# Mixing product of a two-layer kernel: 16 matmuls with 128 weight columns, two at a time, for 32 on 64 by 64, four at a time

## The chip, the cores and the metric

The kernel runs on one core of one Trainium2 chip. The metric is the time of one execution on the device in microseconds (us), where lower is better. Times of instructions come from one profiled execution, recorded by the hardware profiler. An instruction is named by its line in the kernel before: L595 is line 595.

## What is computed

x has the shape (64, 64, 1024): 64 examples, 64 channels, 1024 positions. Two layers are added to it, each of a small condition-dependent product followed by a large one along the positions.

```python
x = x + _L0_ffn_ref(_L0_cond_ref(x, cond_128, ...), L0_ffn_weight)
x = x + _L1_ffn_ref(_L1_cond_ref(x, cond_128, ...), L1_ffn_W, ...)
...
def _L1_cond_ref(x, embedding, W0, b0, W1, b1, W2, b2, weight, bias_k):
    ...
    att = jax.nn.softmax((h @ W2 + b2) / T, axis=-1)
    agg_w = jnp.einsum('bk,koi->boi', att, weight[..., 0])
    agg_b = att @ bias_k
    out = jnp.einsum('boi,bih->boh', agg_w, x) + agg_b[:, :, None]
    return out
```

Layer 0 is a grouped convolution over the positions with a bias from the condition, and an int8-quantised product with a 1024 by 1024 weight. Layer 1 mixes the 64 channels of each example with a 64 by 64 matrix of its own, agg_w[b], and multiplies the result along the positions with a second 1024 by 1024 weight, to which a gated rank-32 product is added. The change is in the mixing, the last einsum that is shown.

## The kernel before

A tile is two examples: 128 partitions (example e of the pair on partitions 64e to 64e + 63, one channel each) by 1024 positions, and there are NT = 32 tiles. The kernel is written out by hand: each engine has one instruction list, and semaphores join the lists. No scheduler moves anything, so the order of the calls in the block of the tensor engine is the order of the work on it.

The block of the tensor engine (from L470) has three parts. The first, to L772, prepares weights and starts the first tiles. The second is the loop of L781, with steps c from 3 to 31. A step has, in this order, the convolution of tile c (`conv`, L541, in float32 for c below 6; `split_conv`, L516, in float16 from there on), the mixing of tile c - 3 (`mix`, L583), the int8 product of tile c - 2 (`int_product`, L611), which is interrupted by small transposes and sums (L620, L624, L564, L691), then the transposes of tile c - 1 (L580) and in every second step a rank product for two tiles (L651 and L656). The third part, from L827, has the last three mixings between pieces of the large product of layer 1 (`dense`, L708), and then the rest of that product for all tiles (L908 and L890), with no mixing in it.

The array of the tensor engine is used in several forms. The profile writes a form as rows*columns: 128*128 is the whole array (L611, L580, L708, L908), 128*64 uses two column halves, one matmul in each (the first half of `split_conv`), 64*64 uses four quarters (the second half of `split_conv`, and `mix`). The quarter follows from the partitions that the operands lie on and from those that the result goes to.

`mix(t)` computes for each example e of the tile the product of x (64 channels by 1024 positions, tile `x1`) with agg_w transposed (64 by 64, tile `mixT`). x1 is the operand that is loaded as weights, and mixT is the one that streams, so that the result comes out with the positions on the partitions, as the large product needs it. For each of 8 blocks k of 128 positions there are four matmuls, for j = 0, 1 (halves of the block, 64 positions each) and e = 0, 1. The result of example e goes to PSUM bank 2 + e, on partitions 64j to 64j + 63. All operands are float32. A float32 matmul stands in the profile as two records, each with its own load of weights, so a `mix` has 32 calls, 64 matmul records and 64 load records; the kernel has 32 of them.

`mix` waits for x1 (`x1_ready`) and for the banks to have been emptied by the scalar engine (`hi_ready`, in the last three tiles `lo_ready`). Its last matmul raises `mix_ready`, on which the scalar engine copies the two banks out.

Of the kernel before, what the change touches and what calls it, by code (L numbers as in the profile page):

```python
# [15 lines left out]
P = 128  # L16
B, CH, L = 64, 64, 1024
# [44 lines left out]
def program(nc, x, x_phases, conv_taps, pack, w_nat, w_rows, w_q, mix_w, mix_rows, w_b, b_ffn, out):  # L62
    ctx = ExitStack()
    with ctx:
        ctx.enter_context(nc.allow_non_contiguous_dma(reason="small weights"))

        def sb(name, shape, dt):
            return ctx.enter_context(nc.sbuf_tensor(name, shape, dt))
# [3 lines left out]
        def sem(name):  # L72
            if name not in sems:
                sems[name] = ctx.enter_context(nc.semaphore(name))
            return sems[name]

        def wait(eng, name, val):
            if val > 0:
                eng.wait_ge(sem(name), val)
# [12 lines left out]
        mixT = mix_home[:, 0:NT * CH].rearrange("p (t o) -> p t o", t=NT)  # L92
# [17 lines left out]
        x1 = sb("x1", [P, 2, L], F32)  # L110
# [96 lines left out]
        def bank(n, k=1):  # L207
            return ps[:, n * 512:(n + k) * 512]
# [262 lines left out]
        def _(pe):  # L471
            mm, tr = nc.tensor.matmul, nc.tensor.transpose
# [110 lines left out]
            def mix(t):  # L583
                if t == 0:
                    pe.wait_ge(sem("agg_ready"), 4)
                wait(pe, "x1_ready", 2 * t + 2)
                if t <= KEPT:
                    wait(pe, "hi_ready", 2 * t)
                else:
                    pe.wait_ge(sem("lo_ready"), 2 * (t - KEPT))  # L590
                for k in range(NL):
                    for j in range(2):
                        for e in range(2):
                            b, l = slice(e * CH, (e + 1) * CH), k * P + j * 64
                            last = mm(bank(2 + e)[j * 64:(j + 1) * 64, k * CH:(k + 1) * CH], x1[b, t % 2, l:l + 64], mixT[b, t, :],  # L595
                                      start=True, stop=True)
                last.then_inc(sem("mix_ready"), 2)

            def int_product(t, h, lo=0, hi=PH):
# [120 lines left out]
            for g in range(GRP):  # L720
                last = mm(ps_small[:, 128 + g * B:128 + (g + 1) * B], pk[:, PACK["w_ctx"]][:, g * P:(g + 1) * P],
                          pk[:, PACK["condT"]], start=True, stop=True)
# [52 lines left out]
            j = 0  # L775
# [5 lines left out]
            for c in range(3, NT):  # L781
# [6 lines left out]
                if c == W_BOUND + 1:  # L788
                    pe.wait_ge(sem("w_max_ready"), 1)
                    wait(pe, "yinv_ready", c)  # L790
                    tr(ps_small[0:1, 160:288], w_max[:, :], ident[:, :]).then_inc(sem("w_top_psum"), 1)
                mix(c - 3)
                if c > W_BOUND + 1:
                    int_product(c - 2, 0, 0, 2)
# [32 lines left out]
            dense(0, 0, 0, 4)  # L827
            batch_total(2)
            mix(NT - 3)
            dense(0, 0, 4, 8)  # L830
            int_product(NT - 2, 0)
            tokens_out(NT - 1)
            int_product(NT - 2, 1)
            dense(0, 1, 0, 5)
            mix(NT - 2)
            int_product(NT - 1, 0)
            int_product(NT - 1, 1)
# [27 lines left out]
            for i in range(4):  # L865
                for k in range(4):
                    q = slice(k * 32, (k + 1) * 32)
                    last = mm(bank(2 + k)[0:R, i * P:(i + 1) * P], limes_n[q, i, :], gateT[q, :], start=True, stop=True)
# [1066 lines left out]
```

## Time and profile before

| | us |
|---|---|
| median of three runs | 615.25 |
| lowest and highest of them | 614.13, 617.0 |
| the profiled execution, its own time | 615.68 |
| its span, first to last instruction | 613.9 |
| tensor engine, matmuls busy | 598.1 |
| tensor engine, weight loads busy | 341.7 |
| vector engine busy | 432.7 |
| scalar engine busy | 357.8 |
| gpsimd engine busy | 375.1 |
| matmuls of L595 (`mix`) busy, 2048 records | 36.4 |
| weight loads of L595 busy, 2048 records | 34.5 |

The span leaves out 1.8 us of the execution's own time, before the first and behind the last instruction. Busy times are unions: where several matmuls run side by side their time is counted once, and the time of a matmul has in it the time that its result takes through the array, which lies beside the next matmuls. So the rate of a stream is read from the starts, or from a group's busy time less one duration, divided by the number of gaps.

### The profile page before, as it was taken

Reading aid. Unit: us, or ns where it says so; the run is one execution under the profiler, and the core shown is the slowest. Engines: PE = TensorE matmul, PEld = TensorE weight load, DVE = VectorE, ACT = ScalarE, POOL = GpSimd, SP = SyncE. Lnnn points to the kernel's source line nnn. Section 1 sums busy time; section 2 is a strip of 40 time slices with the busy share of each in tenths; the row PEclk is TensorE's granted clock in tenths of the full one; section 3 lists DMA queues with packets and bytes.
Section 4 is the critical chain, followed back from the end, with each engine's and each line's share of the span. In section 5 each row is a group of like instructions: output and inputs, shape, how many; then the busy total and the mean of one; then the engine's idle time right before and its main releaser. Section 6 shows DMA issues by size and latency. Waiting matters only on the chain.

```text
span 613.9 us, 16142 instructions
## 1 busy us (share of the span) xinstructions
PE 598.1 (97%) x6455; PEld 341.7 (56%) x6488; DVE 432.7 (70%) x881; ACT 357.8 (58%) x622; POOL 375.1 (61%) x252
## 2 busy tenths in 40 slices
PE   8999999999999999999999999999999999999997
PEld 4656666667777777666554444444444444444443
DVE  6978998988999999986887757754635444335535
ACT  5879998889999999876635244453233333133000
POOL 3336545546776766654888945989787655875200
PEclk9999999999999999999999999999999999999999
DMA  8978987878899999684183025765446443545203
GB/s 335 357 255 298 371 314 261 290 269 316 311 327 328 329 318 324 230 305 140 56 303 125 34 70 202 282 233 190 160 171 207 133 172 140 171 138 171 87 17 137
DMA packets 38344, 136.24 MB, mean 222 GB/s; under 512 B 5004, under 2 KB 5292, under 8 KB 38225
## 3 DMA queue, kind: packets, MB, share of 16 engines
q1 hardware_dynamic: 33518, 118.43, 54.9%
q10 hardware_dynamic: 4752, 16.78, 6.9%
q8 instruction: 52, 0.85, 0.6%
q14 instruction: 22, 0.18, 0.1%
HBM read 87.95 MB, written 47.24 MB: 220 GB/s over the span
## 4 chain that ended last, share of the span: by engine, by line
PE 84%; DVE 3%; issue 2%; ACT 0%; DVEq 0%
PE ps L908 41%; PE ps L611 14%; PE ps L516 8%; PE ps L708 7%; PE ps L595 4%; PE ps L890 2%; PE ps L580 2%; PE ps L656 2%; PE ps L651 1%; DVE yb L1451 1%; PE ps L620 0%; PE ps L624 0%; PE ps L691 0%; DVE w_part L1527 0%; PE ps L676 0%
## 5 line engine op out<-in xcount | busy, mean ns | idle before, releaser
L611 PE MATMUL ps<-wqT,yq_both 128*128 128x512 bf16 x479 | 115.2, 378 | 5.8 <-issue 4.5
L1276 POOL TENSOR_TENSOR x<-x_in,f_all 128x512 f32<-128x512 f32 x64 | 74.4, 1163 | 49.7 <-DVE f_all L1488 49.6
L1280 POOL TENSOR_TENSOR x_split<-x_ph,x_split 128x1032 f16<-128x1032 f32 x25 | 53.7, 2148 | 55.2 <-ACT x_split L989 55.2
L1016 ACT ACTIVATE yv<-yb,yinv 128x128 f32<-128x128 f32 x256 | 77.9, 388 | 0.4 <-DVE yinv L1479 0.4
L1315 POOL TENSOR_TENSOR ring<-ring 128x512 f32<-128x512 f32 x56 | 72.9, 1301 | 4.3
L611 PEld LDWEIGHTS ps<-wqT,yq_both 128*128 128x128 bf16 x512 | 45.5, 99 | 46.2 <-issue 0.8
L1488 DVE SCALAR_TENSOR_TENSOR f_all<-ps,tok_scale,wsc_b 128x512 f16<-128x512 f32 x64 | 47.9, 749 | 18.9 <-PE ps L611 18.1
L516 PE MATMUL ps<-x_split,conv_h 128*64 128x256 f16 (+1 forms) x1248 | 60.1, 274 | 0.1
L516 PEld LDWEIGHTS ps<-x_split,conv_h 128*64 128x64 f16 (+1 forms) x1248 | 47.5, 108 | 9.9 <-issue 7.9
L1059 ACT ACTIVATE ring<-ring,pair_inv 128x1024 f32<-128x1024 f32 x28 | 30.6, 1139 | 36.0 <-DVE wst L1793 11.8
L1806 DVE SCALAR_TENSOR_TENSOR x_in<-ps,unscale,x_in 128x512 f32<-128x512 f32 x30 | 22.5, 750 | 40.8 <-PE ps L908 40.7
L1806 DVE SCALAR_TENSOR_TENSOR wst<-ps,unscale,wst 128x512 f32<-128x512 f32 x28 | 21.0, 750 | 37.4 <-PE ps L908 37.4
L708 PE MATMUL ps<-ffn_wT,ring 128*128 128x512 f16 x192 | 43.3, 379 | 0.0
L1806 DVE SCALAR_TENSOR_TENSOR x<-ps,unscale,x 128x512 f32<-128x512 f32 x28 | 20.9, 748 | 30.8 <-PE ps L908 29.9
L1461 DVE TENSOR_REDUCE rowmax<-yb 128x8 f32<-128x1024 f32 x32 | 39.0, 1219 | 1.3 <-issue 0.3
L595 PE MATMUL ps<-mix_home,x 64*64 64x64 f32 x2048 | 36.4, 219 | 2.4 <-issue 2.4
L994 ACT ACTIVATE yq_both<-ps 128x1024 bf16<-128x1024 f16 x32 | 32.5, 1016 | 9.9 <-PE ps L580 9.7
L595 PEld LDWEIGHTS ps<-mix_home,x 64*64 64x64 f32 x2048 | 34.5, 135 | 4.3 <-issue 3.9
L1451 DVE SCALAR_TENSOR_TENSOR yb<-ps,x_down,ybias 128x1024 f32<-128x1024 f32 x26 | 33.1, 1273 | 3.4 <-PE ps L516 3.4
L989 ACT ACTIVATE x_split<-x_ph 128x1032 f16<-128x1032 f32 x25 | 26.6, 1062 | 13.8 <-PE ps L516 10.3
L1502 DVE TENSOR_SCALAR x_ph<-x_ph,x_up 128x1032 f32<-128x1032 f32 x25 | 30.7, 1229 | 0.3 <-PE ps L825 0.3
L1084 ACT ACTIVATE wsc_b<-ring 128x1024 f16<-128x1024 f32 x7 | 7.4, 1057 | 39.9 <-POOL ring L1315 34.7
(349 smaller groups left out, 1294.3 us busy)
## 6 DMA issues: line engine op xcount, KB each, us to landing
x_in<-in_x SPq DMA_DIRECT2D x32, 512.0 KB, 6.1
x_scratch<-x SPq DMA_DIRECT2D x32, 512.0 KB, 3.6
x_ph<-in_x_phases SPq DMA_DIRECT2D x31, 516.0 KB, 5.1
x_scratch<-ring SPq DMA_DIRECT2D x26, 512.0 KB, 5.4
ring<-x_scratch SPq DMA_DIRECT2D x26, 512.0 KB, 5.3
x_in<-x_scratch SPq DMA_DIRECT2D x12, 512.0 KB, 3.9
out<-x_in ACTq DMA_DIRECT2D x12, 512.0 KB, 3.3
wst<-in_w_rows SPq DMA_DIRECT2D x10, 512.0 KB, 6.7
```

The costliest lines, as they stand in the source:

```text
L516: return mm(ps_conv[o, g * 2 * MB:(g + 1) * 2 * MB], conv_h[k, n, g, w.start + o.start:w.start + o.stop], xp[k, a, g, :, view], start=firs ...
L595: last = mm(bank(2 + e)[j * 64:(j + 1) * 64, k * CH:(k + 1) * CH], x1[b, t % 2, l:l + 64], mixT[b, t, :], start=True, stop=True)
L611: last = mm(acc_bank(t, h), yqT[:, t % 2, p, :], wqT[:, p, h * HALF:(h + 1) * HALF], start=p == 0, stop=p == PH - 1)
L708: last = mm(o, x2_cols[:, x2_slot(n), a, k, :], ffn_wT[:, w, k, h * HALF:(h + 1) * HALF], start=k == 0 and i == 0, stop=k == NL - 1 and i ...
L908: last = mm(b, left(a, k), right(w, k), start=fresh and k == 0 and i == 0, stop=k == 3 and i == 2, skip_group_check=True)
L1016: last = A(yv[:, s, :], yb[:, t % 2, s, :], ACT.Copy, scale=yinv[:, s:s + 1], bias=MAGIC)
L1276: g.tensor_tensor(x1[:, t % 2, s], x_in[:, t % 3, s], f16[:, s], ALU.add).then_inc(sem("x1_ready"), 1)
L1280: g.tensor_tensor(x_split[:, (t - SPLIT) % 2, 1, :], phases(t), x_split[:, (t - SPLIT) % 2, 0, :], ALU.subtract).then_inc(sem("xl_ready"), 1)
L1315: g.tensor_tensor(o, x, y, op).then_inc(sem("s_sum_ready"), 1)
L1451: v.scalar_tensor_tensor(yb[:, t % 2, :, :], sets, x_down[:, t:t + 1], bias, ALU.mult, ALU.add).then_inc(sem("yb_ready"), 1)
L1488: v.scalar_tensor_tensor(f16[:, s], acc_bank(t, h), tok_scale[:, t:t + 1], wsc_b[:, s], ALU.mult, ALU.mult).then_inc(sem("f_ready"), 1)
L1806: v.scalar_tensor_tensor(buf, src, unscale[:, t:t + 1], buf, ALU.mult, ALU.add).then_inc(sem("pair_folded"), 1)
```

## The change

The loop over j is gone. One call now takes the 128 positions of a block as weights (64 rows, 128 columns) in place of two calls with 64 each. The result goes to all 128 partitions of bank 2 + e, which are the same places as before. The two calls for e = 0 and 1 lie on different row halves of the array.

```diff
                 for k in range(NL):
-                    for j in range(2):
-                        for e in range(2):
-                            b, l = slice(e * CH, (e + 1) * CH), k * P + j * 64
-                            last = mm(bank(2 + e)[j * 64:(j + 1) * 64, k * CH:(k + 1) * CH], x1[b, t % 2, l:l + 64], mixT[b, t, :],
-                                      start=True, stop=True)
+                    for e in range(2):
+                        b = slice(e * CH, (e + 1) * CH)
+                        last = mm(bank(2 + e)[:, k * CH:(k + 1) * CH], x1[b, t % 2, k * P:(k + 1) * P], mixT[b, t, :], start=True, stop=True)
                 last.then_inc(sem("mix_ready"), 2)
```

The waits, the semaphores, the DMAs and the instructions of the other engines are the same. On the tensor engine no instruction changes its place against another. The instruction list of the tensor engine in a step of the loop, from the end of the convolution to the int8 product, reads as follows before (64x64 is the shape of the result of a call, partitions by columns; ps is PSUM, mix_home holds mixT, x1 is printed as x):

```order
L516 MATMUL ps<-x_split,conv_h 64x256 [waits f_ready]
L516 MATMUL ps<-x_split,conv_h 64x256 x35
L595 MATMUL ps<-mix_home,x 64x64 [waits hi_ready,x1_ready]
L595 MATMUL ps<-mix_home,x 64x64 x31
L611 MATMUL ps<-wqT,yq_both 128x512 [waits f_ready,yqT_ready]
L611 MATMUL ps<-wqT,yq_both 128x512 x3
L564 MATMUL ps<-x_sum,ones_b 128x1 [waits x_scale_ready,yinv_ready,xsum_ready]
```

The same place of the changed kernel, whose lines from here on are numbered two lower:

```order
L516 MATMUL ps<-x_split,conv_h 64x256 [waits f_ready]
L516 MATMUL ps<-x_split,conv_h 64x256 x35
L594 MATMUL ps<-mix_home,x 128x64 [waits hi_ready,x1_ready]
L594 MATMUL ps<-mix_home,x 128x64 x15
L609 MATMUL ps<-wqT,yq_both 128x512 [waits f_ready,yqT_ready]
L609 MATMUL ps<-wqT,yq_both 128x512 x3
L564 MATMUL ps<-x_sum,ones_b 128x1 [waits x_scale_ready,yinv_ready,xsum_ready]
```

Sixteen calls with 128 result partitions stand where 32 with 64 stood, behind the same waits. In the records, that is 32 loads and 32 matmuls in place of 64 and 64. The form of the array in `mix` is now 64*128, while the half of `split_conv` ahead of it stays 64*64 and the product behind it stays 128*128.

## Rows read from the trace of the kernel before

**Rows 1.** The page, parts 1 and 2: busy time by engine; TensorE's granted clock in tenths

```profile
PE 598.1 (97%) x6455; PEld 341.7 (56%) x6488; DVE 432.7 (70%) x881; ACT 357.8 (58%) x622; POOL 375.1 (61%) x252
...
PEclk9999999999999999999999999999999999999999
```

**Rows 2.** The page, part 4: chain that ended last, by engine

```profile
PE 84%; DVE 3%; issue 2%; ACT 0%; DVEq 0%
```

**Rows 3.** Chain in order of time, two steps of the loop: start us, us, what

```profile
226.71 0.93 PE ps L595 x64
227.64 0.16 issue
227.80 0.38 PE ps L611
...
231.59 0.45 PE ps L580 x8
...
233.59 2.23 PE ps L516 x48
235.83 0.93 PE ps L595 x64
236.76 0.16 issue
```

**Rows 4.** Stretches: busy time of each engine, granted clock, DMA share

```profile
160.00:280.00 120.00, 117.50 (x2270) 84.98 (x2278) 108.08 (x253) 108.75 (x227) 80.14 (x50) 1.00 0.86 304
```

**Rows 5.** Timeline of the weight loads (PEld) in one step: start, busy, what [idle before]

```profile
233.52 1.25 PEld L516 LDWEIGHTS ps<-x_split,conv_h 128*64 128x64 f16 x24 [0.23 <-issue]
234.97 0.59 PEld L516 LDWEIGHTS ps<-x_split,conv_h 64*64 64x64 f16 x24 [0.20 <-issue]
235.55 1.07 PEld L595 LDWEIGHTS ps<-mix_home,x 64*64 64x64 f32 x64
236.69 0.55 PEld L611 LDWEIGHTS ps<-wqT,yq_both 128*128 128x128 bf16 x4
```

**Rows 6.** Line 595, records: duration ns min/median/max, first and last start us, forms

```profile
L595 PEld LDWEIGHTS ps<-mix_home,x x2048: 129/135/135, 39.3 to 308.8; 64*64 64x64 f32 x187
L595 PE MATMUL ps<-mix_home,x x2048: 213/218/268, 39.5 to 308.9; 64*64 64x64 f32 x187
```

**Rows 7.** Line 721, float32 on the whole array, 64 columns streamed: its records

```profile
L721 PEld LDWEIGHTS ps<-pk x8: 190/192/192, 4.9 to 5.8; 128*128 128x128 f32 x8
```

**Rows 8.** Timeline of the weight loads: line 721 without its first load; line 734

```profile
5.08 0.86 PEld L721 LDWEIGHTS ps<-pk 128*128 128x128 f32 x7
...
11.86 0.29 PEld L734 LDWEIGHTS ps<-pair_of,att_rep 64*128 64x128 f32 x2 [0.39 <-issue]
```

**Rows 9.** Line 734, float32 loads on 64 rows by 128 columns: its records

```profile
L734 PEld LDWEIGHTS ps<-pair_of,att_rep x2: 183/185/187, 11.9 to 12.0; 64*128 64x128 f32 x2
```

**Rows 10.** Timeline of the matmuls: line 501, float32, 256 columns streamed; its records

```profile
20.11 1.89 PE L501 MATMUL ps<-x_more,ring 128*128 128x256 f32 x8
...
L501 PE MATMUL ps<-x_more,ring x16: 379/379/382, 16.8 to 21.6; 128*128 128x256 f32 x16
```

**Rows 11.** Line 868, float32 quarters of 32 rows in turn, one column place

```profile
340.37 0.81 PEld L868 LDWEIGHTS ps<-wsc_b,limes_n 32*32 32x32 f32 x32 [0.42 <-issue]
...
L868 PEld LDWEIGHTS ps<-wsc_b,limes_n x32: 101/105/105, 340.4 to 341.1; 32*32 32x32 f32 x32
```

**Rows 12.** Waits of the matmuls, 39 to 340 us: in total, times, longest

```profile
PE ps L595 <- issue: 2.4, 3, 1.2
PE ps L620 <- DVE x_bound L1492: 0.7, 2, 0.5
PE ps L611 <- DVE yb L1451: 0.5, 2, 0.3
```

**Rows 13.** Waits of the weight loads, 39 to 285 us

```profile
PEld ps L516 <- issue: 7.9, 38, 0.2
```

**Rows 14.** Timeline of the matmuls: a mixing with a hole in it

```profile
124.85 0.79 PE L595 MATMUL ps<-mix_home,x 64*64 64x64 f32 x35
126.84 0.69 PE L595 MATMUL ps<-mix_home,x 64*64 64x64 f32 x29 [1.20 <-issue]
```

## The prediction

> **What bounds the kernel now.** I read the busy times first: the tensor engine's matmuls are busy for 598.1 of 613.9 us, and the granted clock is full in every slice, so it is at 2.4 GHz throughout [rows 1]. A busy share of matmuls says little by itself, since matmuls that run side by side and those that wait for a load both count. So I read the chain that ended last: 84% of the span is on the tensor engine, 3% on the vector engine [rows 2]. Followed in order of time, a step of the loop is convolution, mixing, int8 product, transposes, one after the other, with no other engine between them [rows 3]. The other engines are close behind but not ahead: over 120 us of the loop the vector engine is busy for 108.1 and the scalar engine for 108.8 [rows 4]. What the tensor engine waits for others between 39 and 340 us is 0.7 + 0.5 = 1.2 us in four waits, and 2.4 us in three holes inside mixings, for which the profile names no releaser [rows 12, 14]. So whatever the mixing gains or loses in the loop is gained or lost nearly in full, 32 times.
>
> Next: what sets the pace inside a mixing? In the chain it has 0.93 us [rows 3]. Its 64 loads are busy for 1.07 us, each takes 135 ns, so a load starts every (1.07 - 0.135) / 63 = 0.0148 us, or four every 0.059 us [rows 5, 6]. Loads and matmuls come in equal numbers, so both streams have that pace.
>
> **What a load of 128 columns costs.** Line 721 does what the new form does with all 128 rows: float32 weights of 128 columns, 64 columns streamed. Seven loads are busy for 0.86 us and one takes 192 ns: (0.86 - 0.192) / 6 = 0.111 us from load to load [rows 7, 8]. Is it the load or the stream? Line 501 streams 256 float32 columns with the same loads, at (1.89 - 0.379) / 7 = 0.216 us from matmul to matmul; so 64 columns are a stream of 0.054 us, half of what line 721 takes [rows 10]. There the load is the longer one and sets the pace. Fewer rows don't help: the two loads of 64 rows by 128 columns of line 734 are busy for 0.29 us together and take 0.185 each, so they are 0.105 apart [rows 8, 9]. By the durations (192 ns for 128 columns, 135 for 64) a float32 load costs 57 / 64 = 0.89 ns for each column, whatever the rows [rows 6, 7]. In the form of before, 64 columns load in 0.057 us and stream in 0.054: the two are in balance.
>
> That is what the change upsets. Sixteen calls are 32 records. Two at a time they are 16 pairs, and 64 records four at a time were 16 groups of four: the number of beats is the same, but a beat goes from 0.059 to 0.111 us, because each quarter loaded 64 columns and each half now loads 128. The stream gains nothing, since two matmuls run where four ran and there are half as many.
>
> The Trainium skill (TensorE: Matmul & The Clock Gate, on LDWEIGHTS) has the rule that speaks against this change: the time of a load goes by columns and not by rows, columns / 1.2 in ns. By it a load of 128 columns is an estimated 107 ns, and the sum below would be 32 x 15 x 0.004 = 2 us lower than by the row of line 721; the rows agree with it.
>
> **The sum, for one mixing in the loop.** Before, from the first load of a mixing (235.55) to the first load of the int8 product (236.69) there are 1.14 us; the last load of the mixing starts 0.935 into it, which leaves 0.205 behind it [rows 5].
> - After: 15 x 0.111 = 1.665 to the last pair's loads. Behind it 0.205 and some 0.05 more, since a matmul begins when its load is done: 0.255. Together 1.92, so +0.78.
> - Change of form. Before, the mixing had the same form as the end of the convolution and its loads follow without a gap. Where the form changes, loads pause: 0.20 us between 128*64 and 64*64, 38 such pauses of at most 0.2 us with 7.9 in all [rows 5, 13]. The new form, 64*128, differs from both neighbours. The switch behind the mixing was there before (0.205 has it in it), the one ahead of it is new: +0.20. Its ends are 0 (if rows by columns of the same rows count as one form) and 0.4 (if the first load and matmul lie bare as well); I take the row.
> - Five mixings have it already, as other forms stand ahead of them: those of c = 5 and c = 13, and the three behind the loop.
>
> Sum: 27 x 0.98 + 5 x 0.78 = 26.5 + 3.9 = +30.4 us.
>
> **What goes off it.** The holes: three mixings lose 2.4 us in the midst of their records [rows 12, 14]. The engine runs out of instructions there, as I read it, and with half as many in twice the time it would less often. Between none of it and all, I take half: -1.2. The waits for the vector engine: each step is now about 1 us longer on the tensor engine and no longer on the others, so 1.2 us of waits should close: -1.2. Nothing is added elsewhere: the scalar engine gets `mix_ready` 1 us later in a step, and the next mixing and rank product want its copy one step later, 9.1 us in [rows 3]. DMAs are not touched.
>
> Total: +30.4 - 1.2 - 1.2 = +28.0. The profiled execution, 615.68 us, is 0.4 above the median of 615.25; on the median the time is **643.3 us**, 4.6% more.
>
> The other switch is where a rule meets a row. The rows show pauses of 0.20 us at each change of form, before the loads of the new one. The Trainium skill (TensorEngine Tiling, Key Properties) says that a change of tiling mode drains the array and lists 64 by 128 as a mode of its own. By that rule the pause comes with the change; if it didn't, the sum would be 27 x 0.20 = 5.4 us less, 638.
>
> **The rivals.**
> 1. *The halves load one after the other* (chance 0.10). Two 128-column loads on different row halves might share a path that only column places double. Then 32 loads are 0.111 apart: 31 x 0.111 + 0.255 = 3.70 in place of 1.14, +2.56, with the switch +2.76: 27 x 2.76 + 5 x 2.56 - 2.4 = +85, **700 us**. Against it: today loads are 0.0148 apart at 0.057 each, so almost four run at once, which column halves alone would not give; and the 32 loads of line 868, all for one column place and for four row groups in turn, are (0.81 - 0.105) / 31 = 0.023 apart where one of 32 columns takes 0.028 [rows 5, 11]. For it: no row has two 128-column loads on different rows.
> 2. *The halves overlap in part* (0.06): loads overlap one another but a pair must wait for the stream of the one before, 0.111 + 0.054 = 0.165 a beat: 15 x 0.054 = +0.81 a mixing, 32 x 0.81 = +26 more, **669 us**. Line 721, which hides its streams behind its loads, speaks against it.
> 3. *The loads don't pace* (0.04). If the load of 128 columns had a faster way, the beat would stay at the 0.054 of the stream and only the switch be added: 27 x 0.20 - 2.4 = +3, **618 us**, no change by the bound below. The Trainium skill (the same page on TensorE, on Fast Weight Load) has such a way for 128 weights, and excludes FP32. The rows too: 128 columns take 192 ns in float32 [rows 7].
> 4. *Faster* (0.04). The pace is that of the engine's issue: 128 instructions in 1.07 us are now 64, the holes of 2.4 us go, and the new switch costs nothing since the pause comes only with the number of column places. It decides if the beat of a pair is no longer than today's 0.059. Even then two streams at a time have their floor, 16 x 0.054 = 0.86 us against 0.93, so the gain is at most 2.4 + 32 x 0.07 = 4.6; with the holes and half of the rest it is 3.5: **611.8 us**. The holes speak for an issue limit, line 721 against it: with so few instructions it is at 0.111.
>
> That the change does not do what it says can be left out: both halves' operands lie on the partitions 0 to 63 and 64 to 127, and the order of the list is kept.
>
> **How the numbers follow.** The forecast has 0.76. Its own ends: beats of 0.105 (line 734), all holes gone and no switch give 32 x -0.09 = -2.9, -1.2 and -5.4, so 634; a switch of 0.4 gives +5.4 and the holes unchanged +1.2, so 650. The range should hold 8 in 10: it takes all of that, and reaches towards the partly overlapped case, 633 to 660. About 0.5% of 615, or 3 us, is what a measurement of this kernel can tell from no change. Faster by more: rival 4 for the most part, 0.03. Within: the rest of it and rival 3, 0.05. Slower: 0.92.
>
> **What would show it.** Right: the loads of a mixing busy for some 1.85 us with 190 ns for one, starts in pairs about 0.111 apart; a pause of 0.20 ahead of them; the chain's mixing at about 1.8 us plus a gap before and behind; steps of the loop 1 us longer; the clock full; the part behind 341 us unchanged, with vector and scalar engine at a lower share in the loop. The holes: fewer than three. Wrong: loads a pair 0.22 apart (rival 1), 0.165 (rival 2), or 0.06 (rivals 3 and 4); no pause ahead of the mixing; or other waits grown in the loop.

## The result, and the profile after

The changed kernel takes 641.68 us (median of four runs, 641.49 to 642.85) against 615.01 us for the kernel before (median of four as well). The ratio is 1.042, with a 95% interval of 1.040 to 1.044: slower by 4.2%, or 26.7 us. The forecast was 643.3 us, with a range of 633 to 660.

The page of the changed kernel, parts 1, 2 and 4, beside [rows 1, 2]:

```profile
span 639.7 us, 14094 instructions
...
PE 627.4 (98%) x5431; PEld 367.3 (57%) x5464; DVE 437.4 (68%) x881; ACT 359.8 (56%) x622; POOL 375.8 (59%) x252
...
PEclk9999999999999999999999999999999999999999
...
PE 93%; DVE 4%; issue 1%; DMA 1%; SPq 0%; ACT 0%; DVEq 0%
```

The tensor engine has 1024 matmul records fewer and is busy for 29 us more. Its share of the chain that ended last is now 93%. The clock is full throughout, so no part of the loss is a slower clock.

The timeline of the weight loads in one step (start us, busy us, what, idle time before it), which answers to [rows 5]:

```profile
242.08 0.59 PEld L516 LDWEIGHTS ps<-x_split,conv_h 64*64 64x64 f16 x24 [0.20 <-issue]
242.87 1.86 PEld L594 LDWEIGHTS ps<-mix_home,x 64*128 64x128 f32 x32 [0.20 <-issue]
244.80 0.11 PEld L609 LDWEIGHTS ps<-wqT,yq_both 128*128 128x128 bf16 x2
```

The loss stands in the middle row and ahead of it. Its `[0.20 <-issue]` is the new pause of the loads, where [rows 5] had none. The loads are busy for 1.86 us in place of 1.07, and from the first load of the mixing to the first of the int8 product it is 244.80 - 242.87 = 1.93 us in place of 1.14. With the pause, a mixing has grown by 1.00 us (by the starts of the single records 0.795 and 0.205).

The records of the line, which answer to [rows 6], say that a load takes 188 ns in place of 135:

```profile
L594 PEld LDWEIGHTS ps<-mix_home,x x1024: 182/188/188, 39.2 to 334.2; 64*128 64x128 f32 x171
L594 PE MATMUL ps<-mix_home,x x1024: 272/272/320, 39.2 to 334.3; 64*128 64x64 f32 x171
```

So the loads start (1.86 - 0.188) / 31 = 0.054 us apart on average. On one half alone the loads are twice as far apart (0.11 us, shown below by the kernel with the halves in turn), so the two halves do load side by side, in pairs 0.11 us apart.

The chain in order of time, which answers to [rows 3]:

```profile
234.53 1.93 PE ps L594 x32
...
240.71 2.23 PE ps L516 x48
242.94 1.93 PE ps L594 x32
```

The mixing has 1.93 us of the chain where it had 0.93, while the convolution ahead of it still has 2.23.

The waits of the matmuls between 39 and 360 us (in total, times, longest), which answer to [rows 12]:

```profile
PE ps L609 <- issue: 4.6, 29, 0.2
PE ps L689 <- DVE zT L1562: 0.3, 1, 0.3
```

The holes inside mixings are gone, all 2.4 us of them, and so are the waits for `x_bound` and `yb`. The row of L609 was there before with the same size, 4.5 us in 28 waits. It is no wait: matmuls of the int8 product are missing from the records (479 records for 512 loads), and a gap shows where one ran. A second profile of the kernel before has all 512, and no such row.

The part behind the loop did not change. This is the stretch from the last gate work to the end, in the changed kernel:

```profile
366.00:639.70 273.70, 270.02 (x1279) 122.30 (x1277) 141.58 (x191) 81.64 (x83) 169.18 (x106) 1.00 0.43 152
```

and the same work before:

```profile
340.40:613.90 273.50, 269.80 (x1278) 122.26 (x1277) 141.50 (x190) 81.41 (x83) 170.51 (x106) 1.00 0.43 152
```

### The profile page after: what moved, and what is told of

Its sections match the earlier page's. It is cut to its first block, busy times and chain, and to the rows that moved or that the text cites. A ratio compares the mean times of both kernels' runs of the same rounds, so it can differ in the third digit from the quotient of the medians.

```text
span 639.7 us, 14094 instructions
## 1 busy us (share of the span) xinstructions
PE 627.4 (98%) x5431; PEld 367.3 (57%) x5464; DVE 437.4 (68%) x881; ACT 359.8 (56%) x622; POOL 375.8 (59%) x252
## 4 chain that ended last, share of the span: by engine, by line
PE 93%; DVE 4%; issue 1%; DMA 1%; SPq 0%; ACT 0%; DVEq 0%
PE ps L906 40%; PE ps L609 17%; PE ps L594 10%; PE ps L516 9%; PE ps L706 6%; PE ps L888 2%; PE ps L580 2%; PE ps L541 2%; PE ps L654 2%; PE ps L649 2%; DVE wq_max L1374 1%; DMA conv_w<-in_conv_taps 1%; DVE rowmax L1459 1%; PE ps L622 1%; PE ps L618 1%
## 5 line engine op out<-in xcount | busy, mean ns | idle before, releaser
L609 PE MATMUL ps<-wqT,yq_both 128*128 128x512 bf16 x479 | 114.9, 378 | 5.6 <-issue 4.6
L609 PEld LDWEIGHTS ps<-wqT,yq_both 128*128 128x128 bf16 x512 | 45.6, 99 | 46.4 <-ACT yq_both L992 0.7
L594 PE MATMUL ps<-mix_home,x 64*128 64x64 f32 x1024 | 64.1, 275 | 0.0
L594 PEld LDWEIGHTS ps<-mix_home,x 64*128 64x128 f32 x1024 | 59.6, 188 | 7.0 <-issue 6.8
L992 ACT ACTIVATE yq_both<-ps 128x1024 bf16<-128x1024 f16 x32 | 32.7, 1022 | 25.8 <-PE ps L580 25.7
L1004 ACT ACTIVATE ring<-ps 128x512 f32<-128x512 f32 x56 | 29.6, 577 | 3.1 <-PE ps L594 3.1
```

Source lines behind the costliest of these rows:

```text
L594: last = mm(bank(2 + e)[:, k * CH:(k + 1) * CH], x1[b, t % 2, k * P:(k + 1) * P], mixT[b, t, :], start=True, stop=True)
L609: last = mm(acc_bank(t, h), yqT[:, t % 2, p, :], wqT[:, p, h * HALF:(h + 1) * HALF], start=p == 0, stop=p == PH - 1)
```

## Experiments

### How much is the switch, how much the beat: some blocks in the new form

The edit to the kernel before, for the first of two kernels. The second has 4 in place of 7, so that blocks 4 to 7 are in the new form.

```diff
-                for k in range(NL):
+                for k in range(7):
                     for j in range(2):
                         for e in range(2):
                             b, l = slice(e * CH, (e + 1) * CH), k * P + j * 64
                             last = mm(bank(2 + e)[j * 64:(j + 1) * 64, k * CH:(k + 1) * CH], x1[b, t % 2, l:l + 64], mixT[b, t, :],
                                       start=True, stop=True)
+                for k in range(7, NL):
+                    for e in range(2):
+                        b = slice(e * CH, (e + 1) * CH)
+                        last = mm(bank(2 + e)[:, k * CH:(k + 1) * CH], x1[b, t % 2, k * P:(k + 1) * P], mixT[b, t, :], start=True, stop=True)
```

One block:

> Blocks 0 to 6 of each mixing as before (64*64), block 7 in the new form (64*128). Theory (a switch of form costs 0.20 us of pause, and a beat 0.111 in place of 0.059): one switch, inside the mixing, and two long beats: 14 short beats 0.82, pause 0.20, one gap of 0.105, 0.256 behind the last load = 1.38 us from the first load of the mixing to that of the int8 product, against 1.14 before: +0.25 x 32 = +8, less up to 3 for holes and waits: 620 to 623. Rival (the switch is free and all the cost is in beats): 2 x 0.053 x 32 = +3.4, less up to 3: 615 to 618.

Measured: 621.47 us against 616.35 for the kernel before beside it, ratio 1.0085 (1.0054 to 1.0117), inside the forecast and above the rival's 618. Its weight loads in one step:

```profile
237.24 0.59 PEld L516 LDWEIGHTS ps<-x_split,conv_h 64*64 64x64 f16 x24 [0.20 <-issue]
237.82 0.95 PEld L595 LDWEIGHTS ps<-mix_home,x 64*64 64x64 f32 x56
238.84 0.30 PEld L600 LDWEIGHTS ps<-mix_home,x 64*128 64x128 f32 x4
239.21 0.55 PEld L615 LDWEIGHTS ps<-wqT,yq_both 128*128 128x128 bf16 x4
```

Four blocks:

> Blocks 0 to 3 as before, blocks 4 to 7 in the new form. Theory: 8 short beats 0.47, pause 0.20, 7 gaps of 0.111 = 0.78, 0.256 behind: 1.70 us against 1.14: +0.56 x 32 = +18, less up to 3: 630 to 633. With e1 and the changed kernel the time against the number of wide blocks should be a line whose value at no wide block lies some 6 us above the kernel before: that is the switch. Rival (the switch is free): +13.6, less up to 3, 626 to 629, and the line goes through the kernel before.

Measured: 632.6 us against 616.35, ratio 1.0268 (1.0221 to 1.0314), again inside the forecast. Its loads:

```profile
240.72 0.60 PEld L595 LDWEIGHTS ps<-mix_home,x 64*64 64x64 f32 x32
241.39 0.97 PEld L600 LDWEIGHTS ps<-mix_home,x 64*128 64x128 f32 x16
242.43 0.11 PEld L615 LDWEIGHTS ps<-wqT,yq_both 128*128 128x128 bf16 x2
```

A mixing takes 239.21 - 237.82 = 1.39 us in the first, 242.43 - 240.72 = 1.71 in the second, against 1.14 before. The changed kernel has 1.93 and the 0.20 of pause ahead of it. So one, four and eight new blocks cost +0.25, +0.57 and +1.00 us. The step from one to four is 0.107 for each block, and the step from four to eight gives the same. A line through the three points crosses no new block at +0.14: that is what the switch costs net, in 32 mixings 4.5 us and not the 6 that were forecast. (The line is one of rows, not of times: the four executions of the second kernel alone lie 6 us apart.) Inside a mixing the loads stand still for only 0.07 us at the switch, from 237.82 + 0.95 = 238.77 to 238.84, as they do behind every mixing of the kernel before. From the start of the last load of the old form to that of the first of the new one it is 0.20. This takes the place of a beat of 0.11, and the last load of the mixing needs 0.05 more: 0.20 - 0.11 + 0.05 = 0.14. The reading that the switch is free falls, as +0.25 could not be reached by two long beats of +0.053 each.

The profiled execution of the second kernel was its slowest, 636.34 us where the other three took 630.17 to 633.35. It shows what the profiles of the kernel before and of the changed one do not. A hole of 2.62 us stands inside one mixing, and behind it the granted clock is down. The first two rows are the timeline of the matmuls, the last two are stretches, where the number before the DMA share is the clock:

```profile
65.78 0.63 PE L595 MATMUL ps<-mix_home,x 64*64 64x64 f32 x27
69.03 0.43 PE L595 MATMUL ps<-mix_home,x 64*64 64x64 f32 x5 [2.62 <-issue]
```

```profile
60.00:66.00 6.00, 6.00 (x113) 4.62 (x115) 5.58 (x17) 5.78 (x10) 2.39 (x3) 1.00 1.02 374
69.20:76.10 6.90, 6.57 (x34) 3.62 (x33) 0.91 (x2) 2.38 (x5) 0.46 (x2) 0.51 0.50 197
```

For 6.9 us the engine ran at about 1.2 GHz after it had stood nearly idle. The hole and half of these 6.9 us come to some 6 us, and this execution lies 3.0 to 6.2 above the other three, for which there is no profile; so the two can explain most of the distance.

### Do the two halves load side by side: the halves in turn

```diff
-                for k in range(NL):
-                    for e in range(2):
+                for e in range(2):
+                    for k in range(NL):
```

> The changed kernel with the two loops exchanged: the eight calls of example 0, all on one row half, then the eight of example 1. Theory (the two halves load side by side only because neighbouring calls lie on different halves, and matmuls start in order): 31 gaps of 0.111 in place of 15, +1.78 us a mixing, x 32 = +57: about 698. Rival (the engine looks far enough ahead to load the other half, or both halves have a load path of their own that runs free): no more than 5 over the changed kernel's 641.7.

Measured: 701.73 us, ratio 1.138 (1.1327 to 1.1432), 60 us above the changed kernel. Its loads in one step, the whole row and then the loads of it that had started by 197.0 us:

```profile
195.47 3.25 PEld L594 LDWEIGHTS ps<-mix_home,x 64*128 64x128 f32 x32 [0.20 <-issue]
198.79 0.11 PEld L609 LDWEIGHTS ps<-wqT,yq_both 128*128 128x128 bf16 x2
```

```profile
195.47 1.69 PEld L594 LDWEIGHTS ps<-mix_home,x 64*128 64x128 f32 x16 [0.20 <-issue]
```

The time was forecast within 4 us, but not for the reason given, and this is a partial miss. The mixing takes 3.32 us in place of 1.93, which is +1.39 and not +1.78. Within one half the loads are 0.11 apart, as expected. But 7 gaps in the middle, where the list goes over from one half to the other, are 0.055: there loads of the second half go beside the last ones of the first. The other 24 are 0.11, and 24 x 0.1115 + 7 x 0.0555 = 3.06 is the row of 3.25 less one load of 0.188. So the engine looks ahead over a few records, not over a whole row of calls. 32 x 1.39 is 44 us, 16 short of the 60.

The other 16 are the clock. The mean granted clock of this execution is 0.980, and eight stretches stand at half. One of them, and a stretch away from them:

```profile
210.30:213.70 3.40, 3.12 (x10) 1.23 (x11) 0.16 (x1) 2.14 (x4) 0.11 (x1) 0.51 0.96 388
...
160.00:165.00 5.00, 5.00 (x79) 4.60 (x75) 4.56 (x8) 4.26 (x11) 1.68 (x1) 1.00 0.87 299
```

0.02 of the span of 699.1 us is 14 us lost to the clock. The other executions agree: with mean clocks of 0.975, 0.978 and 0.983 they took 703.45, 702.58 and 698.39 us, and all four come to 686 or 687 once that share of the span is taken off; the changed kernel's 641.7 and 44 more are 686. Each of the eight stretches begins within 1 us of the start of the last load of a mixing, in which one half of the array works and the other waits, though the matmuls of such a mixing show as busy without a gap. What the changed kernel has for it: pairs that alternate between the halves, at a full clock. So the order of the calls brings the lower clock with it; that it is the idle half, and why only after eight of the 32 mixings, is not shown.

### Load or stream: 128 columns streamed in the new form

```diff
                 for k in range(NL):
+                    n = 2 if k < NL - 1 else 1
                     for e in range(2):
                         b = slice(e * CH, (e + 1) * CH)
-                        last = mm(bank(2 + e)[:, k * CH:(k + 1) * CH], x1[b, t % 2, k * P:(k + 1) * P], mixT[b, t, :], start=True, stop=True)
+                        last = mm(bank(2 + e)[:, k * CH:(k + n) * CH], x1[b, t % 2, k * P:(k + 1) * P],
+                                  mixT[b, t, :].unsqueeze(1).to_broadcast([CH, n, CH]), start=True, stop=True)
```

> The changed kernel with 128 columns streamed in place of 64 in all calls but the last two (mixT twice; the second copy is written over by the next block, so the result stays the same). Theory (the load of 128 columns sets the beat, and the stream hides behind it): a stream of 0.107 still fits into 0.111: within 2 us of 641.7. Rival (load and stream of a half add up in part): each beat grows by up to 0.054, 15 x 0.054 x 32 = +26: up to 668.

Measured: 642.24 us, ratio 1.0418 (1.0391 to 1.0445); the changed kernel has 641.68, ratio 1.042. The loads of a step:

```profile
243.46 1.86 PEld L595 LDWEIGHTS ps<-mix_home,x 64*128 64x128 f32 x32 [0.20 <-issue]
245.39 0.11 PEld L611 LDWEIGHTS ps<-wqT,yq_both 128*128 128x128 bf16 x2
```

They are busy for 1.86 us as without the second copy. Twice the streamed columns cost nothing, so half of the time in which the array could stream is empty in the changed kernel. The beat is the load's.

### The same in the old form

```diff
                 for k in range(NL):
+                    n = 2 if k < NL - 1 else 1
                     for j in range(2):
                         for e in range(2):
                             b, l = slice(e * CH, (e + 1) * CH), k * P + j * 64
-                            last = mm(bank(2 + e)[j * 64:(j + 1) * 64, k * CH:(k + 1) * CH], x1[b, t % 2, l:l + 64], mixT[b, t, :],
-                                      start=True, stop=True)
+                            last = mm(bank(2 + e)[j * 64:(j + 1) * 64, k * CH:(k + n) * CH], x1[b, t % 2, l:l + 64],
+                                      mixT[b, t, :].unsqueeze(1).to_broadcast([CH, n, CH]), start=True, stop=True)
```

> The kernel before (64*64, four at a time) with 128 columns streamed in place of 64 in all calls but the last four (mixT twice; the second copy is written over by the next block). Theory (the beat is the longer of load and stream, plus about 0.005): load 0.057, stream 0.107, beat 0.111 as in the changed kernel, but without the new switch: 14 x 0.053 = +0.74 us a mixing, x 32 = +24, less up to 3 for holes and waits: 636 to 639. Rival (the beat is set by the count of instructions that the engine issues, so a longer stream hides): within 3 us of 615.

Measured: 634.61 us against 615.67, ratio 1.0311 (1.0281 to 1.0340), 1.4 below the forecast's lower end. The loads of a step:

```profile
202.40 1.78 PEld L596 LDWEIGHTS ps<-mix_home,x 64*64 64x64 f32 x64
204.25 0.11 PEld L612 LDWEIGHTS ps<-wqT,yq_both 128*128 128x128 bf16 x2
```

A mixing takes 1.85 us: +0.71 where 0.74 was forecast. 32 x 0.71 = 22.7, and 3.8 of it are given back; the holes of 2.4 us are part of that, as none of this kernel's mixings has one. In the old form load and stream are in balance, so a longer stream shows in full, and the limit is not the number of instructions issued. The doubled stream here and the doubled load in the changed kernel cost nearly the same. What is left between 634.6 and 641.7 is 7.1 us; by the rows it is 1.93 - 1.85 = 0.08 us and the pause of 0.20 in 27 mixings, and 0.13 in the other five, which take 1.80 here: 27 x 0.28 + 5 x 0.13 = 8.2.

### The type: bf16 operands in both forms

In both kernels the mixing reads only the upper halves of the float32 words, as bf16. The mixing is so computed with less precision; all else is the same. The edit, here to the changed kernel:

```diff
+                x_top = x1[:, t % 2, :].bitcast(BF16).rearrange("p (l w) -> p l w", w=2)[:, :, 1]
+                m_top = mixT[:, t, :].bitcast(BF16).rearrange("p (o w) -> p o w", w=2)[:, :, 1]
                 for k in range(NL):
                     for e in range(2):
                         b = slice(e * CH, (e + 1) * CH)
-                        last = mm(bank(2 + e)[:, k * CH:(k + 1) * CH], x1[b, t % 2, k * P:(k + 1) * P], mixT[b, t, :], start=True, stop=True)
+                        last = mm(bank(2 + e)[:, k * CH:(k + 1) * CH], x_top[b, k * P:(k + 1) * P], m_top[b, :], start=True, stop=True)
```

New form:

> The changed kernel with the mixing's two operands read as bf16, the upper halves of the float32 words, so the mixing is computed in less precision; one record for each call in place of two. Theory (what made the new form dear is that a float32 column costs 0.89 ns to load): 8 beats, each of a bf16 load of 128 columns, whose duration of 99 ns in the int8 product is near that of 40 columns, so a beat of 0.03 to 0.06: 0.2 to 0.4 us from first to last load, with 0.256 behind and the pause ahead: some 0.6 to 0.7 a mixing in place of 1.93: about 605, and the vector and scalar engines show waits of the tensor engine for them. Rival (each column costs the same in any type, 0.89 ns): beat 0.11, 7 x 0.11 + 0.256 = 1.03, about 613.

Old form, with the same two operands in the loops of before:

> The kernel before with the mixing's operands read as bf16 in the same way (upper halves, less precision), in the old form. Theory: 8 groups of four, the beat 0.027 to 0.04 by load and stream of 64 columns at half the float32 price: 0.3 us of loads and 0.2 behind, 0.5 a mixing and no switch ahead: 0.2 us a mixing below e6, so 3 to 7 us below it unless the other engines bound both, 597 to 605. Rival (with half the passes the new form wins, as it has half the instructions): e6 is at or below e7.

Measured: 602.34 us in the new form (ratio 0.9785, 0.9752 to 0.9817) and 601.99 in the old one (0.9782, 0.9755 to 0.9809), beside 615.67. Loads in one step of the new form:

```profile
201.38 0.29 PEld L596 LDWEIGHTS ps<-mix_home,x 64*128 64x128 bf16 x16 [0.20 <-issue]
201.72 0.11 PEld L611 LDWEIGHTS ps<-wqT,yq_both 128*128 128x128 bf16 x2
L596 PEld LDWEIGHTS ps<-mix_home,x x512: 92/93/98, 40.2 to 294.3; 64*128 64x128 bf16 x171
```

and of the old form:

```profile
201.10 0.42 PEld L597 LDWEIGHTS ps<-mix_home,x 64*64 64x64 bf16 x32
201.56 0.11 PEld L613 LDWEIGHTS ps<-wqT,yq_both 128*128 128x128 bf16 x2
L597 PEld LDWEIGHTS ps<-mix_home,x x1024: 103/108/114, 40.0 to 294.1; 64*64 64x64 bf16 x171
```

In float32 the new form takes 0.79 us more for the mixing, in bf16 it takes 0.12 less: 0.34 from the first load to the int8 product against 0.46. The load of 128 bf16 columns takes 93 ns, less than that of 64 columns in the old form with 108. So the rise of the beat belongs to float32: by the starts of the single loads, pairs of the new form and groups of four of the old one are both about 0.03 us apart in bf16. The Trainium skill (TensorEngine Tiling, Restrictions) says that column tiling switches off the fast load of weights; these rows agree, in that only the form without column places has the shorter load (93 ns for twice the columns of 108), and only in bf16.

For the new form 0.6 to 0.7 us a mixing and about 605 us were forecast; it took 0.34 with a pause of 0.20 ahead, and 602.3, so the rival's 613 falls. The loads stayed at the lower end of the theory's 0.2 to 0.4 us, 0.29 - 0.093 = 0.20 from the first start to the last, and behind them it took 0.34 - 0.20 = 0.14 in place of 0.256. The old form was to be 3 to 7 us faster than the new one, and that missed. With its pause of 0.20 the new form is still 0.08 us a step behind, which would be some 2 us in all; the measured difference is 0.35, less than either kernel's executions differ from each other, and the intervals of the two overlap. Between 140 and 250 us the scalar engine is busy for 98% of the time in both (first the new form; the columns after the length are busy times of matmuls, loads, vector, scalar and gpsimd engine):

```profile
140.00:250.00 110.00, 109.08 (x1519) 71.37 (x1520) 103.87 (x253) 107.77 (x223) 79.50 (x50) 1.00 0.91 326
```

```profile
140.00:250.00 110.00, 108.56 (x1745) 72.90 (x1745) 104.02 (x253) 107.98 (x223) 79.71 (x50) 1.00 0.92 327
```

In this stretch the tensor engine no longer sets the pace alone, and that the difference is lost there is how I read it. Both are the only kernels here that beat the one before, at the price of precision in the mixing.

### The holes: the kernel before, profiled again

> The kernel before, unchanged, for a second profile. Theory (the three holes of 0.7 to 1.4 us inside mixings belong to the instruction list, as the engine takes 128 instructions in a us there): holes in the same mixings, those of c = 8, 9 and 13, and about 2.4 us in all. Rival (chance of one execution): holes elsewhere, or of another sum.

Measured: 616.03 us in the one run; its waits between 39 and 340 us:

```profile
PE ps L595 <- issue: 2.3, 4, 1.2
PE ps L620 <- DVE x_bound L1492: 0.9, 3, 0.5
PE ps L611 <- DVE yb L1451: 0.3, 1, 0.3
```

The sum is 2.3 us where it was 2.4, and three of the four holes are in the mixings of before. The long one, 1.20 us at c = 13, is there in both; at c = 8 it is 0.71 in place of 0.46 and at c = 9 0.18 in place of 0.73; the fourth, 0.22 at c = 28, is new. So where the holes fall belongs for the most part to the list and its surroundings, and their size varies. (The row of L595 counts four here and three in [rows 12].) What feeds them is visible in part. In the first profile the hole at c = 13 reaches from 125.64 to 126.84 us [rows 14], and in the 1.2 us ahead of it a block of instructions arrives. These are the DMA queues from 124.4 to 125.6 us (packets, MB, share):

```profile
q1 hardware_dynamic: 113, 0.40, 84.4%
q8 instruction: 1, 0.02, 5.1%
```

The two profiles of the kernel before and those of the two mixed forms hold ten holes of over 0.15 us inside mixings, and in all ten the matmuls go on 1.2 to 1.5 us after such a transfer ended, though one comes only every 5 to 12 us in the loop. The kernel with the doubled stream in the old form issues the same instructions at a longer beat and has no hole; the bf16 kernels, with at most half as many in a mixing, have none either. This speaks for an engine that has run out of instructions, as the prediction read it. No run moved a transfer by itself, so it is not shown.

## Why the prediction was right

The direction, the mechanism and the size hold: 643.3 us forecast, 641.7 measured; +28.0 forecast against +26.7. In the sum for the mixings two small errors add up to less than 1 us, and the terms that go off it were too small.

- **What bounds the kernel.** Right: the chain shows +1.00 us of mixing, and regular steps of the loop are 1.00 us longer: from the first load of a mixing to that of the next 242.87 - 234.46 = 8.41 us, where the same step had 226.43 - 219.02 = 7.41.
- **The beat of a pair, 0.111 us.** Right. The whole stretch was forecast at 1.92 and is 1.93, of which 244.80 - (242.87 + 1.86 - 0.188) = 0.26 lies behind the last load, where 0.255 was forecast. That the load sets it and not the stream is shown by the doubled stream, which cost nothing.
- **The halves load side by side** (rival 1 against it). Right, shown by the loads 0.054 apart and by the kernel with the halves in turn. That kernel's own forecast was right in its sum by two errors that cancelled: a look-ahead that it did not have, and a clock that it took as full.
- **The switch, 0.20.** The pause came as forecast, and a mixing has +1.00 in place of +0.98. But the net cost is smaller. The five mixings that had a change of form ahead of them already took only 1.09 us before (at c = 13 apart from its hole), not 1.14, and grew by 0.84 and not by 0.78. These are the loads of c = 5 and of the int8 product behind it, before and after:

```profile
55.85 1.02 PEld L595 LDWEIGHTS ps<-mix_home,x 64*64 64x64 f32 x64
56.94 0.55 PEld L611 LDWEIGHTS ps<-wqT,yq_both 128*128 128x128 bf16 x4
```

```profile
57.03 1.86 PEld L594 LDWEIGHTS ps<-mix_home,x 64*128 64x128 f32 x32
58.96 0.55 PEld L609 LDWEIGHTS ps<-wqT,yq_both 128*128 128x128 bf16 x4
```

So the new switch is worth 1.00 - 0.84 = 0.16 us, near the 0.14 of the mixed forms. By the starts of the single loads, the second group of four in an old mixing came 0.11 us behind the first in place of 0.06 where the convolution's form went on, and on time where the form had changed: the 0.05 was there without a switch too.
- **The holes, -1.2.** Half of the size: all 2.4 us went. The change has no hole in any of its mixings.
- **The waits for the vector engine, -1.2.** Right in direction and too small. 27 x 1.00 + 5 x 0.84 = 31.2 for the mixings, less 2.4 and 1.2, would be +27.6 in the span, which grew by 25.8. Some steps of before were longer than their matmuls: from one mixing to the next 117.03 - 106.96 = 10.07 us before, and 122.25 - 112.17 = 10.08 for the same two after, though the mixing between them grew by 1.00. The growth filled time in which others had the lead. The rows are the loads of these mixings, before and after:

```profile
106.96 1.07 PEld L595 LDWEIGHTS ps<-mix_home,x 64*64 64x64 f32 x64
117.03 1.07 PEld L595 LDWEIGHTS ps<-mix_home,x 64*64 64x64 f32 x64
```

```profile
112.17 1.86 PEld L594 LDWEIGHTS ps<-mix_home,x 64*128 64x128 f32 x32 [0.20 <-issue]
122.25 1.86 PEld L594 LDWEIGHTS ps<-mix_home,x 64*128 64x128 f32 x32 [0.20 <-issue]
```

- **Rivals 2 to 4** fall by the same rows: a beat of 0.165 or of 0.06 would be a busy time of 2.7 or 1.1 us in the loads, and it is 1.86.

## What to carry to other kernels

Count beats, not instructions: where a matmul takes turns with a load of its own, a tile of the array goes round in the longer of the two (here 0.059 us with 64 float32 columns loaded and 64 streamed, 0.111 with either of them doubled). In float32 the load is priced by its columns, and fewer rows don't make it cheaper; in bf16 both forms went round in about 0.03 us. A wider form halves the calls and halves how many run at once, so it wins only where the load does not grow with it. Look also at which form the neighbours have: each change of form that was added here cost about 0.15 us net, so 27 of them were some 4 of the 26.7 us.

## What the runs showed of the hardware that I had not expected

- With the calls of one half of the array behind those of the other, the granted clock fell although the matmuls showed as busy without a gap: 0.980 on average, half in eight stretches, some 14 us. A hole of 2.62 us in another kernel had the clock at 0.51 for the 6.9 us behind it.
- The pause of the loads at a change of form goes with the stream of the matmul ahead of it: 0.07 us behind the 64 float32 columns of a mixing, 0.20 behind 256 float16 columns, 0.39 behind 256 float32 columns and 0.42 behind 512 float16 columns. The last two stand ahead of these mixings of the changed kernel:

```profile
39.23 1.86 PEld L594 LDWEIGHTS ps<-mix_home,x 64*128 64x128 f32 x32 [0.39 <-issue]
332.55 1.86 PEld L594 LDWEIGHTS ps<-mix_home,x 64*128 64x128 f32 x32 [0.42 <-issue]
```

- The engine overlaps calls on different halves even where they stand some records apart: 7 gaps of 0.055 us at the one place where the list crosses from half to half.
- A bf16 load of 128 columns on one row half takes 93 ns, less than the 108 ns of 64 columns on a quarter.
- Holes of 0.2 to 2.6 us inside mixings with about 120 records per us, ten of ten ending 1.2 to 1.5 us after an instruction transfer: none in the changed kernel, and none in the old form with a longer beat.
